# Two Gelus a hidden unit on ScalarE in place of a rounding copy on GpSimd, in two passes of a four-layer network

## The reference, cut to what matters

```python
x = shortcut + out                     # out: the window attention
h2 = _ln(x, g2, b2)
mlp = jax.nn.gelu(h2 @ w_fc1 + b_fc1, approximate=False) @ w_fc2 + b_fc2
return x + mlp                         # w_fc1: 96 x 384, w_fc2: 384 x 96
```

## Time and profile before

| | us |
|---|---|
| median of 3 runs | 11909.03 |
| lowest and highest | 11908.05, 11911.75 |
| the profiled run | 11907.59 |
| span of the profiled execution | 11905.8 |

### The profile page before, as it was taken

How to read it: one execution, slowest core, us unless ns; L and a number is a source line. 1 busy time by engine, 2 the same in 40 slices (tenths; PEclk the granted TensorE clock), 3 DMA queues, 4 the chain that set the end, 5 groups by cost and what they waited for, 6 DMA issues and landing times. The chain is left out here.

```text
span 11905.8 us, 393166 instructions
## 1 busy us (share of the span) xinstructions
PE 11196.1 (94%) x157972; PEld 8194.0 (69%) x157972; DVE 7361.0 (62%) x12636; ACT 7836.3 (66%) x13524; POOL 4375.4 (37%) x5892
## 2 busy tenths in 40 slices
PE   6999999899999999998989999998999999999999
PEld 3444444577777777777767676766877778777777
DVE  4444444577777777775456666666666666666665
ACT  4555555477777777775346666765777777777776
POOL 0000000377777777774000000001555555555554
PEclk9999999899999999999989999998999999999999
DMA  1111111122222222223643333332010001010000
GB/s 57 36 40 35 40 40 35 36 52 51 51 51 51 51 51 51 51 51 105 215 122 77 76 78 75 78 76 53 24 24 24 24 24 24 24 25 24 24 24 22
DMA packets 1105618, 617.58 MB, mean 52 GB/s; under 512 B 864651, under 2 KB 1076566, under 8 KB 1099704
## 3 DMA queue, kind: packets, MB, share of 16 engines
q1 hardware_dynamic: 1091496, 553.66, 19.2%
q10 hardware_dynamic: 12288, 38.54, 1.0%
HBM read 308.38 MB, written 282.75 MB: 50 GB/s over the span
## 5 line engine op out<-in xcount | busy, mean ns | idle before, releaser
L1485 POOL TENSOR_TENSOR L_HdL<-L_Hd,L_HdH 128x392 fp32r<-128x392 f32 x1536 | 1572.1, 1024 | 283.9 <-POOL L_HdH L1483 283.2
L1469 POOL TENSOR_TENSOR L_SQ<-L_X 96x392 f32<-96x392 f32 x512 | 429.4, 839 | 2316.0 <-DMA L_X<-after_L 2306.4
L985 PEld LDWEIGHTS banks<-L_ident,L_PR 113*113 113x113 f32 x9216 | 1149.4, 181 | 187.9 <-issue 126.8
L985 PE MATMUL banks<-L_ident,L_PR 113*113 113x113 f32 x9216 | 1204.4, 267 | 1.2 <-DVE L_X L1391 0.7
L1220 ACT COPY L_PT<-banks 113x452 f32<-113x452 f32 x1792 | 886.1, 538 | 414.4 <-PE banks L985 414.1
L1236 ACT ACTIVATE L_PR<-L_SX 113x588 f32<-113x588 f32 x1536 | 1087.5, 708 | 51.5 <-DVE L_SX L1363 10.5
L395 PE MATMUL banks<-scan_XS,scan_W1T 97*96 (+1 forms) x2688 | 1113.2, 553 | 0.0
L1533 POOL COPY L_XN<-L_XR 96x392 f32<-96x392 f32 x256 | 147.6, 577 | 2508.2 <-DMA L_XR<-L_norm 2371.3
L1056 PE MATMUL banks<-L_VB,L_PT 113*49 113x34 f32 x36864 | 1063.9, 213 | 1.4 <-ACT L_PT L1220 1.0
L1483 POOL CAST L_HdH<-L_Hd 128x392 fp32r<-128x392 f32 x1536 | 788.6, 513 | 742.8 <-issue 684.1
L1263 ACT ACT_TABLE_LOAD x512 | 656.9, 1283 | 606.2 <-PE banks L992 606.2
(11 more groups left out here) (233 smaller groups left out, 25901.0 us busy)
## 6 DMA issues: line engine op xcount, KB each, us to landing
L_X<-after_L SPq DMA_DIRECT2D x768, 147.0 KB
after_L<-L_X SPq DMA_DIRECT2D x512, 147.0 KB
conv_T<-L_norm_by_phase SPq DMA_DIRECT2D x96, 512.0 KB, 3.3
L_norm_by_phase<-L_XP SPq DMA_DIRECT2D x512, 84.0 KB, 2.1
scan_XT<-in_x SPq DMA_DIRECT2D x33, 1176.0 KB, 7.0
L_norm<-L_XA SPq DMA_DIRECT2D x256, 147.0 KB, 1.9
L_conv<-conv_D ACTq DMA_DIRECT2D x96, 392.0 KB, 3.0
L_XR<-L_norm SPq DMA_DIRECT2D x256, 147.0 KB, 2.4
```

The lines of the kernel that those rows point to most:

```text
L985: mm = pe.transpose(bank(TURN[a])[0:SPAN, (k % 4) * SPAN:(k % 4 + 1) * SPAN], PR[:, st.v if lag else st.u, 2 * k:2 * k + 2, :].rearrange(" ...
L1485: pool.tensor_tensor(HdL[:, u, j].bitcast(F32R), Hd[:, u, j], HdH[:, u, j], ALU.subtract).then_inc(s[f"hd_parts_{j}"], 1)
```

## The change

In `mlp_step`, ACT computes Gelu twice from the same PSUM bank: once into `HdH`, which rounds it, and once into `Hd`. POOL's rounding copy goes; its subtraction waits for both. The signals keep their names: `hd_high_j` now comes from ACT's first Gelu and `gelu_j` from the second. ACT gets a wait for `fc2` with a lag of 4, since the `HdH` that it now writes must have been read by the second matmuls of two chunks before.

```diff
+                def hidden_units(st, j):
+
+                    st.wait(f"fc1_{j}", 2)
+                    unit = bank((7, 6, 7)[j])[:, 0:CH]
+                    act.activation(HdH[:, st.u, j].bitcast(F32R), unit, ACT.Gelu).then_inc(s[f"hd_high_{j}"], 1)
+                    act.activation(Hd[:, st.u, j], unit, ACT.Gelu).then_inc(s[f"gelu_{j}"], 1)
+
...
                         st.wait("hd_parts_2", 4)
+                        st.wait("fc2", 4)
                         for j in (0, 1):
-                            st.wait(f"fc1_{j}", 2)
-                            act.activation(Hd[:, st.u, j], bank((7, 6, 7)[j])[:, 0:CH], ACT.Gelu).then_inc(s[f"gelu_{j}"], 1)
+                            hidden_units(st, j)
                     if st.k:
                         st.wait("heads_t", 1)
                         act.copy(OT[0:C, st.v].rearrange("c (k e q) -> c k e q", k=PAIRS, e=2), window_columns(bank(OT_BANK))).then_inc(s["ot"], 1)
                     if st.m:
-                        st.wait("fc1_2", 2)
-                        act.activation(Hd[:, st.u, 2], bank(7)[:, 0:CH], ACT.Gelu).then_inc(s["gelu_2"], 1)
+                        hidden_units(st, 2)
                         act.preload_act_table_set(LOG_EXP)
...
                         st.wait("fc2", lag + 2)
+                        held(st, f"hd_high_{j}", lag)
                         held(st, f"gelu_{j}", lag)
-                        pool.tensor_copy(HdH[:, u, j].bitcast(F32R), Hd[:, u, j]).then_inc(s[f"hd_high_{j}"], 1)
-                        held(st, f"hd_high_{j}", lag)
                         pool.tensor_tensor(HdL[:, u, j].bitcast(F32R), Hd[:, u, j], HdH[:, u, j], ALU.subtract).then_inc(s[f"hd_parts_{j}"], 1)
```

## The result

| | before | with the change |
|---|---|---|
| median, us | 11910.39 | 12139.26 |
| lowest and highest, us | 11908.05, 11922.95 | 12137.03, 12141.57 |
| runs | 4 | 4 |

The ratio is 1.019, with a 95% interval of 1.0172 to 1.0208: the change makes the kernel slower by 1.9%. Forecast were 12106 us, 197 us more than before; measured are 229 us more. The span of the profiled execution grew by 12139.8 - 11905.8 = 234.0 us.

A forecast was written before the change was run, and what follows sets the result against it. PE and its waits bound the kernel. Keys 0.86 us late less 0.49 us regained at `output` 1 give 0.37 us a step, 189 us over 512 chunks, plus 8 us at loop turns: 12106 us, range 12015 to 12225 (80%).

The forecast's parts named there:

- The bound: Both passes: a step is PE's row of matmuls plus its few waits, from Gelu's table load to the second matmuls.
- The Gelus' starts: On ACT, Gelus and L_OT start 0.385 us apart, making L_OT end at 5.19 and `project` 0.77 us late.
- The keys: On PE, they wait for block 2's second Gelu, which reads their bank 7, and start at 6.03, 0.86 us late.
- POOL's 0.49 us: PE's lateness at `output` 1 from waiting for POOL; dropping POOL's casts gives back the whole 0.49 us a step.
- What is late next: Behind the keys: probabilities ready by 7.99, `turn` 0 at 8.25, 0.2 us to spare; L_LV keeps 0.2 us of its wait.
- The turns of the loop: At 10 turns a pass nothing is given back and `project` is 0.77 us late: 8 us more in all.
- The first one: Rival: the second Gelus hide beside PE's work and POOL's wait of 0.49 us goes: 11658 us; 5%.
- The second one: Rival: 0.45 us idle ahead of the keys is slack, keys only 0.5 us late, time within 0.2% of 11909; 4%.
- The third one: Rival: ACT becomes the bound, starts 0.494 us apart, probabilities or L_LV late too: 12444 us; 9% with what lies between.
- The clock: Rival: PE's clock falls to its lower level for a tenth of the time, 350 us more; 2%.

The follow-up runs named there:

- The run with blocks 0 and 1 alone: Changed kernel with two Gelus only for blocks 0 and 1; block 2 has one Gelu and POOL's cast: 12049.22 us, 1.0115 of the kernel before.
- The run with the extra Gelus alone: Kernel before plus three more Gelus a step on ACT, written to an unread buffer, POOL keeping its casts: 12135.43 us, ratio 1.0189.
- the run with block 2 alone: Changed kernel with two Gelus only for block 2; blocks 0 and 1 have one each and POOL's casts: 11915.65 us, 1.0003 of the kernel before.
- block 1's cast on ACT: Kernel before with block 1's cast moved from POOL to ACT as a rounding copy behind the last Gelu: 11776.63 us, ratio 0.9887.
- The early table load: Kernel before with Gelu's table load moved ahead of ACT's wait for the first hidden units: 11718.18 us, ratio 0.9837.
- the changed kernel with the early load: Changed kernel with Gelu's table load moved ahead of ACT's wait for the first hidden units: 11715.20 us, 0.9834 of the kernel before.

## Why the prediction was right, and where it wasn't

**The bound.** PE's waits between the first Gelu and the second matmuls were where the time came from, in both passes (0.42 us a step in L1, 0.48 in L3, against 0.37 forecast). Right.

**The Gelus' starts.** Forecast 0.385 us apart; from 4011.28 to L_OT at 4012.80 they are 0.38 us apart. The wait for block 0's Gelu was to be 0.6 us and is 0.64, that for L_OT 0.7 and is 0.66, `project` 0.77 us late and is 0.76. Right. The overlap that the Trainium skill's page "ScalarE: Activation LUTs", section "What ACT_TABLE_LOAD costs", states would have given 0.42 us and 12214 us, and doesn't hold for these starts. The 513 ns for one Gelu, the estimate by that page, is near the mean that they have now, 512 ns.

**The keys.** Forecast 0.86 us late, measured 0.92. The term was mis-sized twice, by small amounts: the last Gelu takes 0.53 us, not 0.494, and the keys' load follows its end after 0.11 us (4014.09 to 4014.20), not the 0.06 us that I took from L_OT. I had the latter before me: the last Gelu ended at 5.06 and the keys came at 5.17. Against these two, the last Gelu started 0.03 us earlier than forecast, 2.28 us behind the first. The run with blocks 0 and 1 alone shows that the keys' place is set by that Gelu with the change.

**POOL's 0.49 us.** The size is right to the hundredth: 2.71 us from the keys to `turn` 0 became 2.22. Its cause is not. I put it down to the casts that POOL loses, and said that the whole of it goes by that. The run with the extra Gelus alone has the casts and lost the wait too. PE's own lateness of 0.92 us, less the 0.40 us by which POOL starts later, uses up the wait; the casts' removal gives back nothing that wasn't given by then. As a sum the two are alike, and so the time came out; as a reason it was wrong, and for a smaller delay the two would differ, as the run with block 2 alone shows: one new Gelu of 0.39 us ahead of the keys, and no loss.

**What is late next.** The probabilities were not late, and L_LV kept 0.36 us of its wait, where I had left 0.2. Right, but with less to spare than I wrote. My 0.2 us for the probabilities ran to the first matmul of `turn` 0, while PE waits at its weight load, which stood 0.18 us ahead of it (4007.70 and 4007.88); my own times leave 8.07 - 7.99 = 0.08 us. Measured, L_PR ends at 4003.03 and the load starts at 4003.17, 0.14 us later. With block 1's cast on ACT, which puts the probabilities 0.41 us later, PE did wait for them.

**The turns of the loop.** I added 8 us for 20 turns, which were to be 0.77 us longer each. A loop of 10 iterations turns 9 times, so there are 18. The steps with a turn take 20.92 us in the mean, against 20.25 in L1, and 21.75 against 21.15 in L3: 0.67 and 0.60 us, near what I had. Over and above a step's loss that is some 3 us in all, where I had 8. They vary by more than that between runs. Besides, the first step of L3 takes 16.15 us and not 11.45, 4.7 us once; why is open.

**The rivals.** The first one, that the Gelus hide, did not come, for the reason given: there was no slack ahead of L_OT. The early table load makes slack, and there the second Gelus of blocks 0 and 1 hide, but that of block 2 does not. The second one had the idle time ahead of the keys for slack; it grew from 0.45 to 0.60 us, and took up nothing. The third one needed starts 0.494 us apart, and they came 0.38 us apart. The clock did not change (0.99 in both passes).

## What to carry to other kernels

Ask of a move of work between engines where on the new engine it stands: ahead of or behind the instruction that others wait for. Rounding on ACT cost 229 us for three blocks ahead of it, gained 134 us for one block behind it, and with two blocks and a table load taken off the chain to make room the gain was 369 us, of which the load alone gave 195. Read each pass by itself: on top of the early load the same change gained in the one what it cost in the other. And a wait that a delay elsewhere would have used up can't be counted as a gain: of two halves, run each alone before the sum is made.

## What was not expected of the hardware

A Gelu of 128x392 on ACT takes 494 ns in the kernel before, always (490 to 498 in 452 of them), and 491 to 533 ns in the changed one, the longer ones in the last places: 0.53 us for both of block 2. By place in the row of L1 the means are 498, 492, 503 and 516 ns, then the copy, then 532 and 530 ns. In the run with the change for block 2 alone, and in the changed kernel with the early load, the same two Gelus of block 2 take 497 and 492 ns; there ACT has stood idle behind the copy or ahead of it. So it is neither the block nor its bank, and it goes with how many instructions ACT has done without a pause. Why is open. The copy of 96x392 grew from 482 to 499 ns in the mean with them.

A switch of ACT's tables costs 1.28 us for the load and next to nothing around it: the load starts 0.02 us after the end of the instruction ahead of it (the rounding copy at 4007.42 and the load at 4007.44 in the run with block 1's cast) and the next instruction 0.02 us after it (4008.72 and 4008.74). The Trainium skill's page "ScalarE: Activation LUTs", section "What ACT_TABLE_LOAD costs", gives the same 1283 ns for the load and 1380 ns more for a drain; these rows have no room for the latter.
